# Attention in sub-chunks of 64 tokens, small products as 64-row or 64-column tiles, on one core

## The reference

```python
xn = layernorm(x)
Q, K, V = (xn @ Wq.T), (xn @ Wk.T), (xn @ Wv.T)          # each as (B, L, H, 16)
g = sigmoid(xn_heads @ gw.T); log_c = clip(cumsum(log(g), axis=1), -30, 30)
Gc = exp(log_c) + 1e-6;       R = silu(K @ sw.T)
S = cumsum(K V^T * R / Gc, axis=1) * Gc                   # a 16x16 state per head
attn = (Q . S) @ Wo.T
h = bitlinear(xn, w_fc) + gate * (xn @ v.T @ fast_b.T @ u.T)   # v, u of rank 16; 1024 hidden
out = x + attn + bitlinear(relu(h)**2, w_proj)            # ternary weights times a row scale
```

## Time and profile before

| | |
|---|---|
| runs | 637.47, 638.46, 638.82 us |
| profiled execution, span from the first to the last instruction | 637.8 us |
| PE, PEld (weight loads) busy | 97%, 86% |
| DVE, ACT, POOL busy | 83%, 70%, 61% |
| mean granted clock of TensorE | 0.984 |

### The profile page before, as it was taken

The page is one execution under the profiler, slowest core; times in us unless marked ns, Lnnn a source line. Parts: engine busy times, 40 slices in busy tenths (PEclk is TensorE's granted clock), DMA queues, the critical chain, the costliest instruction groups (busy, mean ns, idle before and its releaser), DMA issues.

```text
span 637.8 us, 21397 instructions
## 1 busy us (share of the span) xinstructions
PE 620.1 (97%) x7710; PEld 545.8 (86%) x7710; DVE 528.7 (83%) x1241; ACT 443.3 (70%) x1036; POOL 387.3 (61%) x505
## 2 busy tenths in 40 slices
PE   7789999999999999999999999999999999999997
PEld 7667888888888888888888888888888888888886
DVE  7678978899888888898789988798988887897863
ACT  4568766677776667776666767775777766677664
POOL 4896666555656665556566565655565665666454
PEclk7689999999999999999999999999999999999999
DMA  9446656886796887866788887668887477775631
GB/s 303 104 97 107 131 106 147 136 145 131 139 147 109 141 138 130 143 133 128 121 145 132 132 146 145 125 106 136 134 143 151 117 137 131 135 130 124 115 54 51
DMA packets 190361, 83.31 MB, mean 131 GB/s; under 512 B 121888, under 2 KB 189728, under 8 KB 190256
## 3 DMA queue, kind: packets, MB, share of 16 engines
q1 hardware_dynamic: 188016, 79.32, 68.4%
q10 hardware_dynamic: 2240, 2.62, 1.3%
HBM read 12.43 MB, written 8.39 MB: 33 GB/s over the span
## 4 chain that ended last, share of the span: by engine, by line
PE 89%; POOL 4%; issue 2%; DMA 2%; SPq 1%; DVE 1%; ACT 1%; ACTq 0%; DVEq 0%; POOLq 0%
PE y_bank L2447 17%; PE attn_bank L2384 9%; PE hid_b L2418 8%; PE hid_a L2418 8%; PE front_b L2313 7%; PE y_bank L2462 7%; PE front_b L2272 7%; PE front_a L2294 6%; PE attn_bank L2397 4%; PE score_a L2346 4%; PE score_b L2346 4%; PE hid_b L2420 2%; PE hid_a L2420 2%; PE score_b L2361 2%; POOL sq_l L821 1%
## 5 line engine op out<-in xcount | busy, mean ns | idle before, releaser
L1871 DVE TENSOR_TENSOR sq_l<-relu_sq,sq_h 128x512 f16<-128x512 f32 x128 | 115.8, 907 | 3.7 <-ACT relu_sq L1162 2.6
L2447 PE MATMUL y_bank<-wproj_t,sq_h 128*128 128x256 f16 x504 | 117.0, 273 | 0.2 <-DVE sq_l L1871 0.2
L2447 PE MATMUL y_bank<-wproj_t,sq_l 128*128 128x256 f16 x504 | 117.0, 273 | 0.0
L1829 DVE TENSOR_TENSOR masked<-score_a,shapes_sb 128x512 f32<-128x512 f32 x128 | 88.2, 689 | 29.6 <-PE score_a L2346 29.0
L1829 DVE TENSOR_TENSOR masked<-score_b,shapes_sb 128x512 f32<-128x512 f32 x128 | 87.5, 684 | 14.0 <-PE score_b L2346 13.7
L746 POOL TENSOR_TENSOR state_diag<-state,state_mask 128x256 f32<-128x256 f32 x56 | 46.8, 836 | 70.7 <-DVE state L1847 34.3
L1153 ACT ACTIVATE sq_h<-relu_sq 128x512 f16<-128x512 f32 x128 | 79.0, 618 | 0.9
L1162 ACT ACTIVATE relu_sq<-relu_sq 128x512 f32<-128x512 f32 x128 | 78.7, 616 | 0.8 <-DVE sq_l L1871 0.7
L2418 PE MATMUL hid_b<-xt,wfc_t 128*128 128x256 f16 x512 | 73.6, 273 | 0.0
L2418 PE MATMUL hid_a<-xt,wfc_t 128*128 128x256 f16 x512 | 73.4, 273 | 0.1
L672 POOL TENSOR_SCALAR xn<-x_sb,neg_mean,rstd 128x256 f32<-128x256 f32 x64 | 42.3, 662 | 50.1 <-DVE rstd L1723 49.9
(11 more groups left out here) (224 smaller groups left out, 1656.9 us busy)
## 6 DMA issues: line engine op xcount, KB each, us to landing
q_diag<-q SPq DMA_DIRECT2D x256, 64.0 KB, 2.8
k_stack<-k SPq DMA_DIRECT2D x128, 128.0 KB, 4.3
x_sb<-in_x SPq DMA_DIRECT2D x32, 256.0 KB, 3.2
out_y<-y_both SPq DMA_DIRECT2D x31, 256.0 KB, 3.2
relu_sq<-in_w_fc ACTq DMA_DIRECT2D x1, 1024.0 KB, 11.5
pj_nat<-in_w_proj ACTq DMA_DIRECT2D x1, 1024.0 KB, 14.2
y_both<-in_w_qk ACTq DMA_DIRECT2D x1, 512.0 KB, 5.1
w_stage<-in_w_qkvz_t SPq DMA_DIRECT2D x1, 512.0 KB, 6.7
```

Of the source, the lines that this page charges most:

```text
L1829: nc.vector.tensor_tensor(masked[:, c, g].rearrange("p (h n) -> p h n", h=4), score_bank[g % 2][:].rearrange("p (h n) -> p h n", h=4), cau ...
L1871: nc.vector.tensor_tensor(sq_l[:, q], sq[:, n], sq_h[:, q], ALU.subtract).then_inc(sq_l_done, 1)
L2447: last = mm(out_part(b, u, c), part[:, q, at:at + P], wproj_t[:, 2 * q + i], start=(q == i == n == 0 and (c == 0 or last_of_all(b, u))), s ...
```

## The change

Attention inside a unit now goes in four sub-chunks of 64 tokens (`SUB`, `SUBS`), with one state for each.

- `scores(c, g)`: four calls a unit in place of eight. Each makes eight products of 64 keys against 128 columns (two heads by 64 queries); the two halves `s` of a chunk go to the two halves of the partitions of one bank. Scores between different halves are no longer computed.
- `mask`: four calls a unit, of the same 128x512.
- `values(c)`: 32 products of 64 rows by 32 columns, 64 tokens long, the halves `s` in two banks.
- `state_updates`: 32 products of 64 rows by 32 columns; its place moves ahead of the scores, and it no longer waits for the masks. `take_updates` on DVE masks them into `own_heads` in two operations, and four `add_state` on POOL sum them into four states, in place of `carry_state` and `diagonal_state`.
- `carried(c)`: eight f32 products of 64x64 on the diagonal of the array, 64 tokens long.
- the low-rank product leaves `hidden(q)`: two `low_rank_part` a unit, of four products of 64 rows each, the two row halves for two banks of hidden values.
- there is one bank for scores and two for attention; `masked` and the states are doubled.
- the order of steps is new on all five engines, in prologue, slots and epilogue.

```diff
+SUB = P // 2
+SUBS = 2
+GROUP = 4
+WAVES = PAIRS // GROUP
...
-        score_bank = [psum("score_a"), psum("score_b")]
-        attn_bank = psum("attn_bank")
+        score = psum("score")
+        attn_banks = [psum("attn_a"), psum("attn_b")]
...   # POOL
+            def add_state(b, u, k):
+                par, c, s = u % 2, k // SUBS, k % SUBS
+                pool.wait_ge(own_done, upto(b, u, SUBS, s))
...
+                    pool.wait_ge(states_done, states_before(b, u, k))
+                    nc.gpsimd.tensor_tensor(to, states[:, par, k], own_heads[:, s, c], ALU.add).then_inc(states_done, 1)
...   # DVE
+            def take_updates(b, u):
+                dve.wait_ge(updates_done, upto(b, u, 1, 0))
...
+                for s in range(SUBS):
+                    chunks = CH if (u, s) != (NU - 1, SUBS - 1) else CH - 1
+                    update = attn_banks[s][:, CH * KT * SUB:CH * KT * SUB + chunks * KT * SUB]
+                    nc.vector.tensor_tensor(own_heads[:, s, 0:chunks].rearrange("p c t n -> p (c t) n"),
+                                            update.rearrange("p (x n) -> p x n", n=SUB),
+                                            state_mask[:].unsqueeze(1).to_broadcast([P, chunks * KT, SUB]),
+                                            ALU.mult).then_inc(own_done, 1)
...   # PE, scores
+                if started(upto(b, u, WAVES * CH, WAVES * c + g) - 1):
+                    pe.wait_ge(mask_done, upto(b, u, WAVES * CH, WAVES * c + g) - 1)
+                for i in range(GROUP):
+                    pair = GROUP * g + i
+                    for s in range(SUBS):
+                        half = slice(SUB * s, SUB * s + SUB)
+                        last = mm(score[half, i * P:i * P + P], k_stack[:, par, pair // KT, c, pair % KT, half],
+                                  q_diag[:, par, pair, :, c * P + SUB * s:c * P + SUB * s + SUB], start=True, stop=True)
...   # PE, values
-                        for q in range(4):
-                            pair = KT * q + half
...
+                        for j in range(4):
+                            pair, r = KT * (2 * (j % 2) + odd) + half, j // 2
+                            at = (pair % GROUP * 2 + r) * SUB
+                            for s in range(SUBS):
+                                rows = slice(SUB * s, SUB * s + SUB)
+                                last = mm(attn_banks[s][32 * j:32 * j + 32, (c * KT + half) * SUB:(c * KT + half + 1) * SUB],
+                                          v_pad[rows, par, c, 8 * half + 2 * j + odd],
+                                          masked[rows, par, c, pair // GROUP, at:at + SUB],
+                                          start=False, stop=False, skip_group_check=True)
...   # PE, carried
+                        for r in range(2):
+                            rows = slice(SUB * r, SUB * r + SUB)
+                            at = c * P + SUB * s
+                            last = mm(attn_banks[s][rows, (c * KT + t) * SUB:(c * KT + t + 1) * SUB],
+                                      states[rows, par, c * SUBS + s, t], q_t[rows, par, t, at:at + SUB],
+                                      start=False, stop=True, skip_group_check=True)
...   # PE, the low-rank part
+                    for side in range(2):
+                        j, rows = 2 * (q + side) + i, slice(64 * side, 64 * side + 64)
+                        mm(hid_bank[side][:, i * UNIT:(i + 1) * UNIT], rank_w[rows, j * P:j * P + P],
+                           z_stack[rows, u], start=(i == 0), stop=False, skip_group_check=True)
...   # PE, slot: the order after
+                attn_projected(*prev)
+                cumulate(*after)
                 values(*nxt, 0)
+                scores(*nxt, 1, 1)
+                keys(*unit_after(b, u, 3))
+                low_rank_part(*nxt, 0)
                 values(*nxt, 1)
                 carried(*nxt, 0)
+                carried(*nxt, 1)
+                hidden(*nxt, 0)
                 projected(b, u, 0)
                 hidden(*nxt, 1)
                 scores(*after, 0, 0)
+                values_gates(*unit_after(b, u, 3), 0)
+                projected(b, u, 1)
+                projected(b, u, 2)
+                low_rank_part(*nxt, 2)
                 scores(*after, 0, 1)
+                values_gates(*unit_after(b, u, 3), 1)
+                projected(b, u, 3)
                 hidden(*nxt, 2)
+                hidden(*nxt, 3)
+                state_updates(*after)
                 scores(*after, 1, 0)
+                queries_t(*unit_after(b, u, 4))
...   # DVE, slot: the order after, from the squares on
+                squares_low(b, u, 2)
+                keys_low(*unit_after(b, u, 3))
                 queries_low(*unit_after(b, u, 3))
+                clip_log(*after)
+                squares_low(b, u, 3)
                 mask(*after, 0, 0)
+                write_factors(*after)
+                stats_of(*unit_after(b, u, 5))
                 mask(*after, 0, 1)
+                waits_for_stats(*unit_after(b, u, 5))
+                moments_of(*unit_after(b, u, 5))
+                scalars_of(*unit_after(b, u, 5))
                 unit_out(*nxt)
+                refine_rstd(*unit_after(b, u, 5))
...   # DVE, slot: its head
+                dens(*after)
+                take_updates(*nxt)
                 log_low(*after)
                 z_low(*after)
+                mask(*nxt, 1, 0)
+                sums_taken(*after)
+                scale_y(*prev)
+                mask(*nxt, 1, 1)
```

More of the change, by code:

```diff
@@ new lines, in prologue @@
+                sums_taken(0, 3)
+                squares_low(0, 2, 0)
+                refine_rstd(1, 2)
+                keys_low(1, 0)
+                queries_low(1, 0)
+                z_low(0, 3)
+                clip_log(0, 3)
+                write_factors(0, 3)
+                mask(0, 3, 0, 0)
+                unit_out(0, 2)
+                scale_y(0, 1)
+                mask(0, 3, 0, 1)
+                squares_low(0, 2, 1)
+                take_updates(0, 3)
+                dens(1, 0)
@@ L2543, in prologue @@
                 values(0, 0, 1)
+                carried(0, 0, 0)
+                queries_t(0, 2)
+                cumulate(0, 1)
+                carried(0, 0, 1)
+                keys(0, 2)
+                projected(0, 0, 1)
                 scores(0, 1, 0, 0)
-                cumulate(0, 1)
-                queries_t(0, 2)
-                carried(0, 0, 1)
+                values_gates(0, 2, 0)
+                low_rank_part(0, 1, 0)
+                scores(0, 1, 0, 1)
                 hidden(0, 1, 0)
-                scores(0, 1, 0, 1)
@@ L2550, in prologue @@
-                scores(0, 1, 0, 2)
-                keys(0, 2)
-                projected(0, 0, 0)
-                scores(0, 1, 0, 3)
-                projected(0, 0, 1)
+                hidden(0, 1, 1)
+                values_gates(0, 2, 1)
+                projected(0, 0, 2)
+                state_updates(0, 1)
                 scores(0, 1, 1, 0)
+                projected(0, 0, 3)
+                values(0, 1, 0)
                 scores(0, 1, 1, 1)
-                values_gates(0, 2, 0)
-                scores(0, 1, 1, 2)
@@ L2559, in prologue @@
-                values_gates(0, 2, 1)
-                scores(0, 1, 1, 3)
-                hidden(0, 1, 1)
+                low_rank_part(0, 1, 2)
+                queries_t(0, 3)
+                values(0, 1, 1)
                 hidden(0, 1, 2)
-                values(0, 1, 0)
-                state_updates(0, 1)
-                values(0, 1, 1)
                 carried(0, 1, 0)
-                queries_t(0, 3)
                 cumulate(0, 2)
-                projected(0, 0, 2)
+                hidden(0, 1, 3)
@@ L2580, in prologue @@
-                values_gates(0, 3, 1)
-                hidden(0, 2, 0)
-                scores(0, 2, 1, 1)
-                scores(0, 2, 1, 2)
-                attn_projected(0, 0)
-                scores(0, 2, 1, 3)
-                queries_t(1, 0)
-                values(0, 2, 0)
-                state_updates(0, 2)
+                values_gates(0, 3, 1)
+                projected(0, 1, 0)
+                projected(0, 1, 1)
+                state_updates(0, 2)
+                hidden(0, 2, 1)
@@ L2589, in prologue @@
+                scores(0, 2, 1, 0)
+                values(0, 2, 0)
+                queries_t(1, 0)
+                carried(0, 2, 0)
+                low_rank_part(0, 2, 2)
+                cumulate(0, 3)
+                scores(0, 2, 1, 1)
+                projected(0, 1, 2)
                 values(0, 2, 1)
-                carried(0, 2, 0)
-                cumulate(0, 3)
-                hidden(0, 2, 1)
+                keys(1, 0)
                 carried(0, 2, 1)
-                keys(1, 0)
@@ L2634, in prologue @@
                 hidden(0, 3, 3)
-                scores(1, 0, 1, 2)
-                values_gates(1, 1, 1)
-                scores(1, 0, 1, 3)
-                attn_projected(0, 2)
```

(9 more changed lines are left out.)

988 lines of the change are left out of this document (463 added, 525 removed).

## The result

The changed kernel takes 655.22 us (median of four runs, 651.12 to 657.81), the kernel before beside it 638.64. The ratio is 1.0253, 95% interval 1.0214 to 1.0292: 2.5% slower, where 625 us was predicted. The runs also scatter more, 6.7 us against 1.6.

A forecast was written before the change was run, and what follows sets the result against it. The prediction took PE, a queue of matmuls without gaps, to bound the kernel; 0.43 us gained a unit times 31 gives 13 us, span 637.8 to 624.8, about 625 us, own range 615 to 634, 8 in 10 within 594 to 658.

The forecast's parts named there:

- part 3: Values on PE: 1.74 us a unit becomes 0.91 with eight tiles at once, gain 0.83; other bound a loss of 0.08.
- part 4: State updates on PE: 0.45 us stays with eight tiles at once, 0.91 with four; a mean of 0.045 us more.
- The predicted gain of 0.43: Sum of the six parts on PE, in us gained a unit.
- issue is the floor: Rival: 14 ns per instruction is PE's pace, not the columns'; 1.3 us a unit worse, 665 us; chance 0.05.
- part 6: Changes of tile shape on PE: 15 a slot, 0.09 to 0.095 us each, plus bare first weights; loss 1.56 us a unit.
- Scores: Scores on PE: column halves run side by side, 1.74 us a unit becomes 0.91, gain 0.83.
- Low-rank pairs: Low-rank product on PE: row halves overlap, 0.87 us a unit becomes 0.44, gain 0.44; nil if they don't.
- Carried: Carried on PE: two diagonal tiles at once, mean 0.79 us becomes 0.86, loss 0.07; 1.7 us without overlap.
- (a) to (d): Possible new waits: scores for mask, values(0) for take_updates, state_updates for unit_out, carried for adds; none expected, nothing added.
- The start: First 52 us, not bound by PE, in new order: no gain or loss, within 4 us.

The follow-up runs named there:

- the short bursts: PE alone, computation left out, short bursts of small products on zeros behind 64 full-array products: 32 calls of f32 halves take 0.79 us, 64 f16 pairs 0.62.
- the scores alone: Kernel before with only its scores as pairs of 64-column tiles, 12 changes of shape in a slot: 681.04 us, ratio 1.0664.
- the old start: Changed kernel with the start's order of the kernel before on all four engines, slots untouched: 653.51 us, ratio to before 1.0205.
- one pass: Values and state updates read as bf16 upper halves, one load-and-matmul pair for two: 622.47 us in the changed kernel, 630.57 in the kernel before.
- the bursts here: PE alone, computation left out, long bursts of small products on zeros, each behind eight full-array products: PE stood for 62 of 167 us.

## Why the prediction was wrong

**The step that failed** is part 3 with part 4, "with all eight at once 8 groups of 0.057" and "the issue distance of 7 ns gives 64 x 7 ns = 0.45, so it does not forbid eight". Eight at once is right. But the 7 ns came from seven loads and were applied to bursts of 64 pairs, while PE holds that pace for 32 pairs only. By the short bursts a call is 0.18 us longer, three a unit, 0.55. The predicted gain of 0.43 becomes a loss of 0.12; the quiet units show 0.07 to 0.10. My rival "issue is the floor" had the right place, but priced at 14 ns a pair throughout (a loss of 1.3 a unit) and given 0.05.

**The bursts of 128x32 tiles in the kernel before** hid this: at 28 and 14 ns a pair the array is slower than the supply (8 ns). The short bursts of whole rows confirm it, 64 pairs without a bend in 1.03 us.

**Shape changes** (part 6): 15 a slot, 0.09 to 0.1 each into 64x128, 128x64 and 64x32 tiles, confirmed in the trace and, with 0.11 to 0.12, by the scores alone. **Scores**: 0.35 a call; side by side as assumed. **Low-rank pairs**: side by side, and worth 0.24 us a unit in place. **Carried**: two diagonal tiles at once, 1.08 us for two calls against 1.05. **Waits**: none of (a) to (d) came in every slot; one of 0.5 us for a mask stands in the whole trace, and PE's idle time in the 27 units grew by 1.3 us.

**The start**, put at nothing within 4 us, lost 4.6 in the profiled execution at the first `hidden`. The runs with the old start leave its worth in the changed kernel between nothing and some 6 us; it stays open how much of it the queues behind would have taken up.

**Stops for instructions** were in no part of the prediction. Not every wait that the profile puts down to `issue` is one. The five of the changed kernel, 4.2 us, stand at products that wait for no semaphore, four of them inside bursts of small products; from start to start they are longer still, since the modelled ends cover the first of each (1.13 us from 316.38 to 317.51, 0.91 counted). The four of the kernel before, 4.2 us too, stand ahead of steps that wait for something: `group_sums`, `fc_weights` for GpSimd, and twice the first scores of a unit for moves. So it shows no stop. Counted in the same way, the changed kernel with the old start has 5.2 us of stops and the one with low-rank products of 128 rows 5.0; the scores alone in half columns (8222 pairs) and the kernels with one pass (9022 or 6238 pairs) have none, but for one of 0.6 us. They come where bursts of 64 small pairs do, which fits *fetch*. That they are also the reason why the changed kernel's runs scatter by 6.7 us was a guess that the runs don't bear out: the changed kernel with one pass and the old start shows no stop and scatters by 10.1 us.

The sum, with the terms as measured, for the profiled execution: 31 x 0.07 to 0.10 = 2.2 to 3.1 for the units, 4.6 at the start, 5.2 for the stops (1.46, 0.45, 1.13, 0.48 and 1.84 us from start to start, less the ordinary distances), and 3.3 less than before for PE's other waits between the first `hidden` and the thirtieth `attn_projected` (1.5 against 4.8 us). That is 8.7 to 9.6 of the 11.5; the other 2 to 3 us stay open. Against the forecast, a span of 624.8, the queue is the largest term: 31 x 0.5 = 15.5 of 24.5 us. The median lies 4 us above that execution.

## What to carry to other kernels

Cutting a product into smaller tiles trades columns for instructions: before counting on it, compare the length of the longest unbroken burst with PE's 32 pairs, and the pairs per microsecond over a long stretch with the supply (128 pairs in 3.45 to 4 us in the bursts here). Count changes of tile shape at 0.1 us each and put steps of one shape side by side. A pace read from a few instructions holds for a few instructions; ask how long a row must be to carry the step that is built on it.

## What was not expected of the hardware

- PE starts 32 pairs within 0.12 us, 3.9 ns apart (f16, 64 columns, eight tiles; 0.24 us with the change of shape), and after 32 pairs falls to 8.3, with a hole of 0.1 us between. The slower pace is the same at either clock of the array.
- In f32 at full clock the pace after the 32nd pair is 8 to 10 ns for halves of 64 columns; why it isn't 8.3 throughout stays open.
- PE can use up its instructions: 128 pairs between stops, and over 1024 pairs 25 to 29 ns a pair. In the changed kernel, with bursts of 64 pairs, such stops of 0.5 to 1.8 us from start to start appear in five places.
